# Layer 0's attention in pairs of steps, and layer 1's first norm inside layer 0's feed-forward

## What is computed

```python
# layer 0 attention, on layernorm(x); 16 heads of 8 features
Qp = query @ Wq + bq;  K = l2norm(key @ Wk + bk);  V = value @ Wv + bv;  Q = l2norm(Qp)
attn = softmax(Q K^T * SCALE);  out = (attn V) @ Wo + bo
x += layernorm(out + Qp) * ln_gamma + ln_beta
# layer 0 feed-forward: 8 experts of width 256, gates of the top 2 (all 8 experts are computed)
z = layernorm(layernorm(x), ln_g, ln_b);  x += layernorm(x) + sum_e gate_e * (gelu(z W1_e + b1_e) W2_e + b2_e)
# layer 1 attention, on layernorm(x), with ternary weights and inputs rounded to 8 bits by ONE scale per tensor
i_scale = max(|x|) / 127;  qx = round(x / i_scale)
vis = bitnet(ctx, W_d2v);  image = bitnet(vis, W_img);  fused = bitnet(layernorm(x), W_txt);  ...
```

## Time and profile before

| what | value |
|---|---|
| time, median of 3 runs | 1656.27 us (1655.55 to 1656.34) |
| the profiled execution's own time | 1655.02 us |
| its span | 1653.2 us |
| busy: PE, PEld | 1430.5 us (87%), 1013.6 us (61%) |
| busy: DVE, ACT, POOL | 986.8 us (60%), 938.7 us (57%), 650.0 us (39%) |
| largest group of layer 0's attention: exponentials L853 | x128, 141.6 us busy, mean 1114 ns |
| its weighted sums L773 | x1024, 83.3 us busy, mean 398 ns (four run side by side) |
| its scores L759 | x256, 65.8 us busy, mean 512 ns (two run side by side) |
| second products of the feed-forward L1243 | x512, 62.5 us busy, mean 275 ns |

### The profile page before, as it was taken

The page is one execution under the profiler, slowest core; times in us unless marked ns, Lnnn a source line. Parts: engine busy times, 40 slices in busy tenths (PEclk is TensorE's granted clock), DMA queues, the critical chain, the costliest instruction groups (busy, mean ns, idle before and its releaser), DMA issues. The chain is left out here.

```text
span 1653.2 us, 30254 instructions
## 1 busy us (share of the span) xinstructions
PE 1430.5 (87%) x9781; PEld 1013.6 (61%) x9791; DVE 986.8 (60%) x2435; ACT 938.7 (57%) x1928; POOL 650.0 (39%) x685
## 2 busy tenths in 40 slices
PE   2999996996776366999999879789999999999995
PEld 2444445985454255776777556567777777777764
DVE  3566645757665545676666446466666666666651
ACT  1577784774564534666665433256666656666652
POOL 3254434000000052656655412246456456465541
PEclk8799997998898577999999989889999999999998
DMA  4300000000000041000000000000000000000002
GB/s 133 90 1 0 0 1 26 1 1 1 1 0 1 2 116 33 1 1 0 0 0 1 1 1 1 1 0 2 1 1 0 0 0 0 0 0 0 1 2 77
DMA packets 29766, 20.47 MB, mean 12 GB/s; under 512 B 9489, under 2 KB 26744, under 8 KB 29688
## 3 DMA queue, kind: packets, MB, share of 16 engines
q1 hardware_dynamic: 28536, 18.95, 4.1%
q10 hardware_dynamic: 1152, 0.52, 0.1%
HBM read 18.42 MB, written 1.05 MB: 12 GB/s over the span
## 5 line engine op out<-in xcount | busy, mean ns | idle before, releaser
L1833 POOL TENSOR_TENSOR l3a_prob<-l3a_prob,l3a_rinv 128x512 f32<-128x512 f32 x256 | 260.4, 1040 | 199.8 <-DVE l3a_rinv L2061 196.5
L1993 ACT ACTIVATE l3a_prob<-l3a_scores_ps,l3a_nmax 128x512 f32<-128x512 f32 x256 | 173.3, 683 | 134.2 <-DVE l3a_nmax L2055 134.2
L2055 DVE TENSOR_REDUCE l3a_nmax<-l3a_scores_ps 128x2 f32<-128x1024 f32 x128 | 150.8, 1219 | 83.2 <-PE l3a_scores_ps L1879 83.1
L853 ACT ACTIVATE l0a_prob<-l0a_scores_ps,l0a_k_scale 128x1024 f32<-128x1024 f32 x128 | 141.6, 1114 | 53.0 <-PE l0a_scores_ps L759 52.9
L1833 POOL TENSOR_TENSOR l2a_prob<-l2a_prob,l2a_rinv 128x512 f32<-128x512 f32 x128 | 130.0, 1040 | 88.3 <-DVE l2a_rinv L2061 87.9
L1892 PE MATMUL l3a_turned_ps<-const,l3a_prob 128*128 128x128 f32 x1024 | 156.2, 275 | 3.3 <-DVE l3a_probT L2067 1.2
L1892 PEld LDWEIGHTS l3a_turned_ps<-const,l3a_prob 128*128 128x128 f32 x1024 | 118.2, 141 | 27.2 <-DVE l3a_probT L2067 11.9
L1993 ACT ACTIVATE l2a_prob<-l2a_scores_ps,l2a_nmax 128x512 f32<-128x512 f32 x128 | 86.8, 684 | 70.7 <-DVE l2a_nmax L2055 70.7
L1903 PE MATMUL l3a_work_ps<-l3a_probT,l3a_v 128*64 128x256 f32 x1024 | 124.7, 385 | 1.6 <-ACT l3a_probT L2000 0.9
L2067 DVE COPY l3a_probT<-l3a_turned_ps 128x512 f32<-128x512 f32 x128 | 87.8, 686 | 51.4 <-PE l3a_turned_ps L1892 51.4
L1903 PEld LDWEIGHTS l3a_work_ps<-l3a_probT,l3a_v 128*64 128x64 f32 x1024 | 68.3, 136 | 51.8 <-issue 23.6
(11 more groups left out here) (623 smaller groups left out, 3601.7 us busy)
## 6 DMA issues: line engine op xcount, KB each, us to landing
l1f_w<-in_L_ffn_w SPq DMA_DIRECT2D x16, 256.0 KB, 2.8
load_ctx_rows<-in_ctx SPq DMA_DIRECT2D x1, 1536.0 KB, 7.5
l3f_experts_w<-in_L_ffn_W SPq DMA_DIRECT2D x24, 64.0 KB, 1.9
w_l_w<-in_L_ffn_W SPq DMA_DIRECT2D x1, 1024.0 KB
out_x<-x_tokens SPq DMA_DIRECT2D x8, 128.0 KB, 1.9
const<-in_constants SPq DMA_DIRECT2D x1, 589.0 KB
w_l_wo<-in_L_xattn_Wo SPq DMA_DIRECT2D x1, 512.0 KB
l0f_raw_f<-in_L_xattn_W_f SPq DMA_DIRECT2D x1, 512.0 KB, 4.1
```

The source lines that it names most:

```text
L853: e.activation(prob[n % 4][:, :], sc[n % 2][:, :], ACT.Exp, scale=kscale[:, n % KT:n % KT + 1]).then_inc(m.prob_ready, 1)
L1833: e.tensor_tensor(prob[n][:, :], prob[n][:, :], bcast(rinv[:, n:n + 1], [P, S]), ALU.mult).then_inc(m.prob_ready, 1)
L1993: e.activation(prob[at][:, :], bank(u), ACT.Exp, bias=nmax[:, at:at + 1], accum_out=rsum[:, at:at + 1]).then_inc(m.exp_ready, 1)
L2055: e.tensor_reduce(nmax[:, at:at + 2], sps[:, i * 1024:(i + 1) * 1024].rearrange("p (h k) -> p h k", h=2), AX.X, ALU.max, negate=True).then ...
```

## The change

In layer 0's attention TensorE's order becomes pairs: the scores of two steps, the weighted sums of two steps, and then the side work of two steps. The side work changes its slots (the queries first, then the keys and values; the tokens of batch b+2 at the end of turn b), and so do the copies on VectorE and ScalarE and the order on GpSimd. The norm of a batch is made a turn earlier and is split into statistics and application. The residual is made in two operations on GpSimd: `residual_next` beside the next queries, and a copy of it (a product with ones) once the last one has been read. The prologue makes batch 1's norm and tokens, two scores and no more.

In the feed-forward the chunk c-1 gets layer 1's norm during chunk c: statistics at its expert 2, application at 3, transposes and ScalarE's copy at 5, the largest element at 6; the last chunk's follows at the end. The sum of each image projection is accumulated by the activation that copies it, in place of VectorE's reduction. Both scales are found at the end of the feed-forward's block, with two more fillings of `chain`. The stages "l1a_norm" and "l1s_in" go.

```diff
@@ l0_attention, GpSimd @@
+            def next_residual(b):
+                wait(e, m.residual_ready, b)
+                e.tensor_tensor(residual_next[:, :, :], qp[:, :, :], bcast(g.l0_bo[:, :].unsqueeze(1), [P, TPB, D]),
+                                ALU.add).then_inc(m.residual_next_ready, 1)
             def keep_residual(b):
                 wait(e, m.y_kept, b)
-                e.tensor_tensor(residual[:, :, :], qp[:, :, :], bcast(g.l0_bo[:, :].unsqueeze(1), [P, TPB, D]),
-                                ALU.add).then_inc(m.residual_ready, 1)
+                e.wait_ge(m.residual_next_ready, b + 1)
+                e.tensor_tensor(residual[:, :, :], residual_next[:, :, :],
+                                bcast(g.ones[:, 0:1].unsqueeze(2), [P, TPB, D]), ALU.mult).then_inc(m.residual_ready, 1)
...
                 if after:
+                    square_q(b + 1)
+                    q_norms(b + 1)
                     square_k(b + 1)
-                    front.gpsimd(e, b + 1)
                     k_low(b + 1)
-                    if after_that:
-                        fix_c(b + 2)
-                keep_residual(b)
                 if before:
                     finish(b - 1)
+                keep_residual(b)
+                if after:
+                    next_residual(b + 1)
+                if before:
+                    update(b - 1)
+                if after_that:
+                    fix_c(b + 2)
                 if after:
                     k_scales(b + 1)
-                if before:
-                    update(b - 1)
+                if after_that:
+                    front.gpsimd(e, b + 2)
                 if after:
-                    square_q(b + 1)
-                    q_norms(b + 1)
                     keep_v(b + 1, True)
@@ l0_attention, TensorE @@
+            def between(b, n):
+                before, after, after_that = parts(b)
+                if n == STEPS:
+                    if after_that:
+                        tokens(n, b + 2)
+                    return
+                if before and n == 1:
+                    turn_pv(n, b - 1, 3)
+                if after and n == 2:
+                    queries(n, b + 1)
+                if before and n == 3:
+                    turn_o(n, b - 1)
+                if after and n == 4:
+                    keys(n, b + 1)
+                if before and n == 5:
+                    output(n, b - 1)
+                if n in (6, 9, 13):
+                    turn_pv(n, b, (6, 9, 13).index(n))
+                if after and n == 7:
+                    values(n, b + 1)
+                if after and n in (8, 11, 12, 15):
+                    turn_keys(n, b + 1, (8, 11, 12, 15).index(n))
+                if after and n in (10, 14):
+                    turn_queries(n, b + 1, (10, 14).index(n))
             def turn(b):
...
+                for n in range(1, STEPS, 2):
+                    for k in (n + 1, n + 2):
+                        if k < STEPS:
+                            scores(b, k)
+                        elif after:
+                            scores(b + 1, k - STEPS)
+                    weighted(b, n - 1)
+                    weighted(b, n)
+                    between(b, n)
+                    between(b, n + 1)
...
             scores(0, 0)
+            scores(0, 1)
+            turn_queries(8, 0, 1)
+            turn_keys(9, 0, 3)
+            tokens(10, 1)
             turns(e, turn)
@@ l0_attention, ScalarE: copies after the exponential of step n @@
+                    if n == 1 and after:
+                        keep_z(b + 1, 0)
+                    if n == 5 and before:
+                        keep_o(b - 1)
+                    if n == 9 and after:
+                        keep_v(b + 1, 1)
@@ l0_attention, VectorE: the new turn @@
+                    if n == 0 and before:
+                        keep_kS(b, 3, 1)
+                    if n == 1 and before:
+                        keep_pv(b - 1, 3)
                     if n == 2 and before:
                         divide(b - 1, 3, 1)
                     if n == 3 and after:
+                        keep_q(b + 1, 0)
+                    if n == 4:
+                        keep_pv(b, 0)
+                    if n == 5 and after:
+                        clamp_q(b + 1)
+                        keep_k(b + 1)
                         k_high(b + 1)
+                    if n == 6 and before:
+                        add_qp(b - 1)
+                    if n == 7:
+                        divide(b, 0, 0)
+                        if after:
+                            split_q(b + 1)
                         if before:
                             norm_y(b - 1)
+                    if n == 8:
                         keep_pv(b, 1)
+                    if n == 9 and after:
+                        keep_kS(b + 1, 0, 0)
+                        clamp_k(b + 1)
                     if n == 10:
                         divide(b, 1, 1)
+                    if n == 11 and after:
+                        keep_qS(b + 1, 0, 0)
+                    if n == 12:
                         if after:
+                            keep_kS(b + 1, 1, 1)
+                        keep_pv(b, 2)
                     if n == 13:
                         if after:
+                            keep_kS(b + 1, 2, 0)
+                        if after_that:
+                            norm_statistics(b + 2)
                     if n == 14:
                         divide(b, 2, 1)
+                    if n == 15:
+                        if after:
+                            keep_qS(b + 1, 1, 0)
+                        if after_that:
+                            norm_apply(b + 2)
@@ before turn 0, VectorE @@
+            norm_statistics(1)
+            norm_apply(1)
             turns(e, turn)
@@ l0_ffn, TensorE @@
+                if x == 5 and c >= 1:
+                    turn_next(c - 1)
...
+            turn_next(CHUNKS - 1)
+            turn_last()
+            spread_last()
@@ l0_ffn, ScalarE @@
+            def keep_next(c):
+                e.wait_ge(m.aux_filled, aux_filled(c, "next"))
+                e.activation(l1.zT[:, c * CW:(c + 1) * CW], aux[:, :], ACT.Copy).then_inc(m.next_zT_ready, 1)
...
+                e.activation(img[:, k * S:(k + 1) * S], chain[:, :], ACT.Identity, scale=out_scale[:, 1:2], bias=g.l1_bimg[:, 0:1],
+                             accum_out=l1.avg[:, k:k + 1]).then_inc(m.projected_kept, 1)
@@ l0_ffn, VectorE @@
-                e.tensor_reduce(l1.avg[:, k:k + 1], img[:, k * S:(k + 1) * S], AX.X, ALU.add).then_inc(m.top_ready, 1)
...
+                if x == 2 and c >= 1:
+                    next_statistics(c - 1)
+                if x == 3 and c >= 1:
+                    next_apply(c - 1)
+                if x == 6 and c >= 1:
+                    next_top(c - 1)
...
+            next_statistics(CHUNKS - 1)
             img_top(B - 1)
+            largest_part(2, l1.img_top[:, :])
+            next_apply(CHUNKS - 1)
+            next_top(CHUNKS - 1)
+            largest_part(3, l1.top[:, B:B + CHUNKS])
+            largest_last()
+            keep_last_scales()
@@ l1_attention: the block "l1a_norm" and this line go @@
-        activation_scales(nc, g, "l1s_in", [l1.img_top[:, :], top[:, 0:AllTiles.BANKS]], [scales(IMG), scales(Z)])
```

264 lines of the change are left out of this document (134 added, 130 removed).

## The result

| | before | after |
|---|---|---|
| median (lowest to highest) | 1655.91 us (1655.35 to 1656.34) | 1632.34 us (1631.68 to 1634.26) |
| runs | 4 | 4 |
| profiled execution, its span | 1655.02, 1653.2 us | 1631.68, 1629.8 us |
| busy: PE, DVE | 1430.5, 986.8 us | 1404.0, 997.2 us |
| busy: ACT, POOL | 938.7, 650.0 us | 934.4, 658.3 us |

The ratio is 0.986, 95% interval 0.9843 to 0.9877: 23.6 us less, where 19.9 were forecast. Both spans split at the same places of the program. In the last column the prediction's norm part stands as it divides on these places: 1.3 of transposes and 0.6 of an added maximum, less 1.5 by which the update was to end sooner, lie in the feed-forward, the rest behind it.

A forecast was written before the change was run, and what follows sets the result against it. TensorE was taken to set the attention's pace, VectorE and hops between engines the feed-forward's end. Terms -13.6 + 1.0 - 0.8 - 6.5 = -19.9 from 1655.0, plus 1.25, gave 1636 us; range 1620 to 1650.

The forecast's parts named there:

- The pairs on TensorE: Layer 0's attention: each pair of steps saves 0.49 us, eight pairs 3.9; TensorE and ScalarE alone give a 20.8 us turn.
- rival A: Layer 0's attention: the turn is TensorE's and ScalarE's alone, 20.8 us, total 1623 us; chance 0.25.
- The copies and holds: Attention turn: VectorE's in-order queue, held behind GpSimd, adds 2.2 us to 20.8; turn 23.0, six turns gain 13.6.
- Turn 0: Attention's start: TensorE waits for batch 1's norm, going on 4.4 us later; pairs save about 3.4; charged +1.0 us.
- The last turn: Attention's end: little side work, paced by the exponentials, 17.0 us becoming 16.2, so -0.8 us.
- The norm's part: Layer 1's norm and scales: all but a quarter of the norm stage moves into the feed-forward; net -6.5 us.
- Rival D: Attention turns: waits drop TensorE to half the clock, turn 27.1 us, total 1661 us; chance 0.05.

The follow-up runs named there:

- three kernels worked out above: The change (1632.34 us), the change with GpSimd's residuals at the start of its turn (1625.27 us), and all attention alterations together (1619.39 us).
- run with the residuals first: The change with GpSimd's two residual operations moved to the start of its next turn, behind the values' pad: 1625.27 us (0.9813).
- the best kernel: The change with altered prologue, residuals at the start of GpSimd's turn, square of k behind the finish, VectorE's order turned round: 1619.39 us (0.9774).
- prologue run: The change with GpSimd's prologue work put behind the first queries' split and batch 1's norm moved to split and keys' copies: 1627.28 us (0.9818).
- the part alone: The change with layer 0's attention as before, keeping the layer-1 norm, scales and feed-forward of the change: 1649.19 us (0.9956).

## Why the prediction was right

**The pairs on TensorE.** Right in kind and in size. Two scores start to start take 0.66 us (forecast 0.43 + 0.21 = 0.64), two weighted sums 1.00 as forecast. Side work came out at 7.2 us a turn, as 9.26 less the 1.00 wait and eight savings of 0.13 had given; there two small errors meet. The six turns before have a mean of 25.26, but a steady one is 25.55 us, so the side work before was 8.4 and not 8.3, and a pair saves 0.16. The exponentials delay two pairs by 0.5 in sum, as forecast. The turn without waits is 20.9 to 21.0 us in the three kernels worked out above, for 20.8. So rival A had the floor right too; what it left out is VectorE's queue.

**The copies and holds.** The mechanism stood where the prediction put it: TensorE waits before the second weighted sum's turning and before the queries', released by VectorE, with the variance at 1.28 and the splits long. The size was 22.77 - 20.9 = 1.85 us, for 2.2 taken, and what it is made of was partly luck. The holds themselves are 2.8 us a turn. The variance was held 1.11 us (forecast 1.2). Of the 2.2 put in front of the split only 0.80 came, as the scaling of the queries passed beside GpSimd's finish unheld (0.48 us). One hold the forecast had missed (k_high beside the square of k, 0.85), but that one fills time in which VectorE would wait for TensorE's output product. And 0.30 of the 1.85 stand before the keys' turning, by the rows above a wait for `k_low` itself, which the prediction did not have. The run with the residuals first shows the 0.80 of the splits as 0.80 of a turn; for the variance's 1.11 no run does, since where its hold went away another came.

The rule of the Trainium skill that the prediction weighed ("SBUF — State Buffer", "Who interferes with whom") holds further than I used it. It also says that only operations which need the shared pair are held: casts and scalings from SBUF in the two-port modes, and sums of two SBUF inputs, but no reduction. The trace agrees: VectorE's reduction L937 takes 0.67 beside GpSimd's product at 91.90, as anywhere else, and the copies out of PSUM in the rows above are no longer than alone. Being able to be held is not yet being held, though: the scaling of the queries is an operation of that kind and passed beside GpSimd's power (0.76 us on two elements) in 0.48, but took 1.26 beside the square of k in the best kernel. Reading it so tells in advance where GpSimd's work may stand; the run with the residuals first is that reading put to use.

**Turn 0** was the failed term: +1.0 forecast, -1.25 measured. TensorE went on at 53.67, after a wait of 3.81 us, and scores followed at 54.26; the prediction's 53.6 had the transposes inside it, so the chain was 0.7 us longer than forecast. What the prediction charged wrongly was the time behind it. In the kernel before, the granted clock rose to 2.4 GHz at about 60.7, and in the change at about 57.9. Columns as in the earlier trace rows, the clock is the third number from the end (1.00 for 2.4 GHz, 0.50 for 1.2); first before, then the change:

```profile
60.00:62.00 2.00, 2.00 (x18) 0.83 (x14) 1.19 (x3) 1.45 (x3) 0.37 (x1) 0.82 0.00 0
```

```profile
56.00:58.00 2.00, 2.00 (x20) 0.96 (x12) 0.00 (x0) 1.22 (x2) 0.00 (x0) 0.53 1.16 238
58.00:60.00 2.00, 2.00 (x24) 0.93 (x23) 0.43 (x2) 1.27 (x2) 0.61 (x1) 1.00 0.29 55
```

2.8 us less at half the clock are 1.4 us of TensorE's work (an estimate from the two clock levels), out of the 2.25 between forecast and measurement; the rest, 0.85, lies in what the pairs of turn 0 save (3.4 had been put) and wasn't taken apart. The prologue run shows that the wait itself still costs its length; in it the clock rises 4.7 us sooner too (at about 53.2), so the rise went with the place where TensorE took up its work.

**The last turn.** The difference came as forecast (-0.7 for -0.8), but by luck: the prediction took 245.91 + 1.07 for the end of the last weighted sums, and in the kernel before one more starts at 247.19 and ends at 247.83. The stretch was 17.86 us and not 17.0, and is now 17.14 and not 16.2.

**The norm's part** came as forecast: 10.8 us behind the start of the last update, and -6.3 in the traces, -7.0 for the part alone, -6.5 forecast. How the feed-forward's +0.7 divides is only half shown. The transposes and what goes with them cost 1.7 us, by the run with all chunks at the end (1.3 was put for the transposes); the sums taken off VectorE give 1.2 to 1.6 back, by the run with the sums back (1.5). The half clock moves as much: the same feed-forward code took 132.4 us in one trace (8.2 us of it at half the clock), 134.6 in the change (13.0) and 135.4 in another (15.4), and the kernel before had 12.1 us of it.

**Rival D** (half clock in the attention) did not come in the change, which shows a granted clock of 1.00 in its steady turns with waits of 1.16 us. It did come in the run with k_low twice, from 2.18 us of wait a turn, as the last section shows.

## What to carry to other kernels

Where VectorE's queue is what the next matmul waits for, look at its short operations on SBUF and what GpSimd does beside them, and move GpSimd's work to where VectorE reads PSUM, reduces or waits; a move that only changes which operation is held gives nothing (0.07 us of a steady turn, against 0.80 for the right place). After an edit that turns an order round, add up the pair before and after the wait: a wait that vanishes in one row and comes back in the next has only moved. Measure a wait from start to start against the same step without one: here idle times of 0.18 and 0.22 us cost 0.8. And a chain of small steps behind a stage is worth cutting by chunks into it, even if the stage's bounding engine pays for them (1.7 us paid, 10.8 saved).

## What was not expected of the hardware

**A wait of 2.2 us can cost a spell of half clock.** The change and the run with k_low twice, each in three stretches (columns as in the earlier trace rows, the clock is the third number from the end):

```profile
94.00:98.00 4.00, 4.00 (x42) 2.50 (x38) 3.48 (x13) 3.46 (x5) 1.80 (x4) 1.00 0.01 4
98.00:102.00 4.00, 3.92 (x45) 1.92 (x44) 2.27 (x5) 3.76 (x5) 1.19 (x2) 1.00 0.00 0
102.00:106.00 4.00, 4.00 (x40) 2.69 (x39) 2.09 (x7) 3.04 (x4) 1.12 (x2) 1.00 0.00 0
```

```profile
94.00:98.00 4.00, 1.82 (x14) 1.59 (x16) 3.90 (x7) 1.52 (x2) 3.92 (x4) 1.00 0.00 0
98.00:102.00 4.00, 3.99 (x30) 1.83 (x26) 3.93 (x10) 2.12 (x2) 3.22 (x5) 0.57 0.01 2
102.00:106.00 4.00, 4.00 (x51) 2.21 (x47) 3.25 (x9) 3.51 (x4) 1.91 (x3) 1.00 0.01 4
```

TensorE ran at 1.2 GHz behind four of the seven waits of about 2.1 us (the longest spell from about 173.4 to 180.2, in the turn of 26.6 us), and after the three others it stayed at 2.4 GHz, with waits of the same length. The seven waits are 15.0 us in sum, but TensorE's waits for the weighted sums' copies fell from 8.2 to 3.9 us in return, so the waits leave a good part of the 18.8 us to the half clock: some 20 us of this attention ran at it behind those waits, which is about 10 us of TensorE's work (an estimate from the clock shares of the trace). Its turns took 24.5 to 26.6 us, the longest with the longest spell. What decides whether such a wait is followed by a spell was not tried.

**Outside the changed code the clock moves the time by some us.** The five runs with the residuals at the end of the turn took 1625.0, 1625.3, 1627.5, 1630.2 and 1630.3 us, those with the square late as well 1625.4 twice and 1630.6 to 1630.9 three times. The profiled run of the former has a span 6.4 us below the change's, of which 1.8 lie in the attention, 2.2 in the feed-forward, whose code is untouched and where the granted clock is 0.97 instead of 0.95, and 2.4 behind it. What selects it was not tried. It is why the verdicts on single steps above rest on turns and on the start of the last weighted sum, and not on the medians alone.
